# Interleaving the two matrix products of an expert loop on TensorE

## What is computed

```
glog = xf @ Wg + bg            ; 2 of 4 groups are kept
elog = xf @ We + be            ; 4 of 8 experts are kept in each group
h = gelu(xf @ W1[g] + b1[g])   ; 192 -> 768
o = h @ W2[g] + b2[g]          ; 768 -> 192
y = y + o * combine            ; sum over the experts that a token chose
```

## Time and profile before

| what | value |
|---|---|
| median of 3 runs | 839.55 us (836.72 to 843.9) |
| profiled execution, own time | 850.15 us |
| its span | 848.3 us |
| PE busy in the span | 722.8 us (85%) |
| expert loop, first product to the last | 452.08 to 839.01 us of the span |

### The profile page before, as it was taken

One profiled execution on the slowest core, in us unless ns is written; L12 is line 12 of the kernel. 1 busy time (PEld: TensorE's weight loads), 2 busy tenths in 40 slices (PEclk: granted clock), 3 DMA queues, 4 the chain that ended last, 5 costly groups with the idle time before them and its releaser, 6 DMA issues.

```text
span 848.3 us, 19851 instructions
## 1 busy us (share of the span) xinstructions
PE 722.8 (85%) x6412; PEld 603.1 (71%) x6412; DVE 397.9 (47%) x1167; ACT 239.4 (28%) x672; POOL 299.2 (35%) x259
## 2 busy tenths in 40 slices
PE   4967958788978999787267999999999999999995
PEld 4944645546663598575236888889889988898895
DVE  5657445653564714894892333333333333333332
ACT  2102212122415401111232333333333333333332
POOL 0122016021022420261003545545545555464554
PEclk9977867768976899796567999999999999999998
DMA  8940000000000002003112574546454556545422
GB/s 214 232 87 2 1 3 2 2 1 3 1 1 0 1 2 113 0 1 112 26 36 88 168 234 114 138 107 162 98 155 103 157 154 165 147 103 154 106 45 40
DMA packets 35163, 69.49 MB, mean 82 GB/s; under 512 B 6598, under 2 KB 21543, under 8 KB 35111
## 3 DMA queue, kind: packets, MB, share of 16 engines
q0 software_dynamic: 15840, 17.71, 12.2%
q10 hardware_dynamic: 8352, 34.30, 11.7%
q1 hardware_dynamic: 10919, 16.74, 7.5%
HBM read 58.75 MB, written 9.98 MB: 81 GB/s over the span
## 4 chain that ended last, share of the span: by engine, by line
PE 57%; DVE 16%; DMA 11%; issue 8%; POOL 2%; ACT 2%; POOLq 1%; ACTq 0%; DVEq 0%; SPq 0%
PE bank L1475 11%; PE bank L1467 9%; DMA arena<-normed_rows,fetch_u 7%; PE bank L1470 6%; PE bank L1250 4%; DMA out_dram<-arena,number_u 3%; PE bank L1324 3%; PE bank L1204 3%; PE bank L1452 2%; PE bank L1339 2%; PE bank L1363 2%; PE bank L1270 2%; PE bank L1208 1%; PE bank L1317 1%; PE bank L1298 1%
## 5 line engine op out<-in xcount | busy, mean ns | idle before, releaser
L618 POOL DMA_INDIRECT out_dram<-arena,number_u x80 | 127.1, 1588 | 31.6 <-issue 21.4
L612 POOL DMA_INDIRECT arena<-normed_rows,fetch_u x80 | 78.3, 979 | 150.3 <-DMA out_dram<-arena,number_u 54.2
L1169 DVE COPY arena<-bank 128x256 f32<-128x256 f32 x81 | 34.4, 424 | 161.9 <-PE bank L1452 146.6
L784 ACT ACTIVATE arena<-bank,arena 128x128 f32<-128x128 f32 x234 | 66.0, 373 | 123.3 <-PE bank L1470 110.7
L1475 PE MATMUL bank<-arena 128*128 128x192 f32 x468 | 85.4, 329 | 4.0 <-DVE arena L1189 2.8
L1475 PEld LDWEIGHTS bank<-arena 128*128 128x128 f32 x468 | 75.0, 190 | 7.3 <-ACT arena L784 3.7
L524 POOL TENSOR_SCALAR rstd<-mv 128x4 f32<-128x4 f32 x12 | 2.7, 228 | 201.7 <-DVE mv L860 201.7
L1467 PE MATMUL bank<-arena 128*128 128x128 f32 x468 | 60.4, 279 | 0.9 <-issue 0.2
L1467 PEld LDWEIGHTS bank<-arena 128*128 128x128 f32 x468 | 56.2, 191 | 5.7 <-issue 4.7
L784 ACT ACTIVATE arena<-bank,w_space 128x128 f32<-128x128 f32 x132 | 37.3, 373 | 72.6 <-PE bank L1470 71.8
L552 POOL TENSOR_TENSOR arena<-arena,v_space 128x2304 f32<-128x2304 f32 x8 | 34.5, 4316 | 55.4 <-DVE arena L1108 50.1
(11 more groups left out here) (237 smaller groups left out, 1265.5 us busy)
## 6 DMA issues: line engine op xcount, KB each, us to landing
arena<-in_moe_w_dram ACTq DMA_DIRECT2D x15, 579.0 KB
arena<-in_moe_w_dram ACTq DMA_DIRECT2D x15, 576.0 KB
w_space<-in_moe_w_dram ACTq DMA_DIRECT2D x7, 579.0 KB
w2small<-in_moe_w_dram ACTq DMA_DIRECT2D x7, 579.0 KB
w_space<-in_moe_w_dram ACTq DMA_DIRECT2D x7, 576.0 KB
wab<-in_moe_w_dram ACTq DMA_DIRECT2D x7, 576.0 KB
arena<-in_xf_dram SPq DMA_DIRECT2D x8, 480.0 KB, 15.8
arena<-in_w_dram SPq DMA_DIRECT2D x8, 450.0 KB, 14.2
```

What stands on the lines that cost most here:

```text
L612: pool.indirect_dma_start(out=mo_stage[:, s * ROWN:(s + 1) * ROWN], out_offset=None, in_=normed_rows, in_offset=bass.IndirectOffsetOnAxis( ...
L618: pool.indirect_dma_start(out=out, out_offset=bass.IndirectOffsetOnAxis(ap=number_u[:, s:s + 1], axis=0), in_=mo_res[:, s * D:(s + 1) * D] ...
L784: nc.scalar.activation(mo_hT[:, m, :], bank[2 + m][:, 0:P], ACT.Gelu, bias=b1[:, m:m + 1]).then_inc(free[2 + m], 1)
L1169: nc.vector.tensor_copy(mo_xT.rearrange("p k t -> p (k t)"), bank[1][:, 0:2 * P]).then_inc(free[1], 1)
```

## The change

One step of PE's loop handles two tiles: the second products of tile i-1, placed between the first products of tile i. Six second products, three before the first products and three among them; the 64-row products, which were six in one row, come in three pairs (m = 0,1; 2,3; 4,5), each pair behind full-height products. The first step multiplies a cleared `mo_hT` (POOL clears it before the loop), and six second products stand behind the last step. As tile i-1 may belong to the expert before, the second weights of the four places become one tile, `mo_w2_all`, and the place is added from a register of PE, `w2_at`. The loads of the weights move from ACT's queue to SP's and go when the last tile of the expert before has had its second products. At the beginning the second weights of experts 0 and 1 are loaded later, since their new place is used by the third attention until then. ACT loses one wait and DVE waits for one more count of `full[0]`.

```
-        mo_w2 = [w2_space[:], w2small[:, 0:W2N]] + [view(P, W2N) for _ in range(2)]
+        mo_w2_all = view(P, AHEAD * W2N)
+        mo_w2 = [mo_w2_all[:, u * W2N:(u + 1) * W2N] for u in range(AHEAD)]
...
             for u in range(2):
-                load_expert(sp, u, u)
+                load_first(sp, u, u)
             was_read(sp, "D", "proj", T - 1)
-            load_expert(sp, 2, 2)
+            for u in range(AHEAD):
+                if u >= 2:
+                    load_first(sp, u, u)
+                load_second(sp, u, u)
...
+            sp.wait_ge(sem("table_ready"), 1)
+            for e in range(1, NE - AHEAD + 1):
+                first = expert_start(sp, e, 1)
+                sp.wait_ge(full[0], first + (moe_base[0] + 1))
+                sp.sem_inc(sem("loading"), 1)
+                load_first(sp, (e - 1) % AHEAD, e + AHEAD - 1)
+                load_second(sp, (e - 1) % AHEAD, e + AHEAD - 1)
...
+            was_read(pool, "D", "proj", T - 1)
+            nc.gpsimd.memset(mo_hT.rearrange("p m t -> p (m t)"), 0.0).then_inc(sem("hidden_clear"), 1)
...
-                    act.wait_ge(full[0], first + moe_base[0])
-                    load_expert(act, (u + AHEAD - 1) % AHEAD, e + AHEAD - 1)
...
-                    act.wait_ge(full[0], i + moe_base[0])
...
-                    added, summing = dve.snap(i + 1), dve.snap(i + (moe_base[0] + 1))
+                    added, summing = dve.snap(i + 1), dve.snap(i + (moe_base[0] + 2))
...
+            def second(m):
+                rhs = mo_w2_all[:, bass.ds(pe.snap(w2_at, min_val=0, max_val=(AHEAD - 1) * W2N) + m * D, D)]
+                ins = mm(bank[0][:, 0:D], mo_hT[:, m, :], rhs, start=(m == 0), stop=(m == MC - 1))
+                if m == MC - 1:
+                    ins.then_inc(full[0], 1)
+
+            def first_rows(w1e, m):
+                mm(bank[2 + m][:, 0:P], w1e[:, m * P:(m + 1) * P], mo_xT[:, 0, :], start=True, stop=False)
+
+            def last_rows(w1e, m):
+                for q in (m, m + 1):
+                    r, c = q % 2 * REST, HID + q // 2 * P
+                    mm(bank[2 + q][:, 0:P], w1e[r:r + REST, c:c + P], mo_xT[r:r + REST, 1, :], start=False, stop=True).then_inc(full[2 + q], 1)
...
+                pe.reg_mov(w2_at, (e - 1) % AHEAD * W2N if e else 0)
                 with pe.Fori(first, end) as i:
+                    pe.wait_ge(free[0], i + (moe_base[0] - 1))
+                    for m in range(3):
+                        hidden_read(i, m)
+                        second(m)
                     pe.wait_ge(free[1], i + (moe_base[1] + 1))
...
+                    first_rows(w1e, 0)
+                    first_rows(w1e, 1)
+                    last_rows(w1e, 0)
+                    hidden_read(i, 3)
+                    second(3)
+                    first_rows(w1e, 2)
+                    hidden_read(i, 4)
+                    second(4)
+                    first_rows(w1e, 3)
+                    last_rows(w1e, 2)
+                    hidden_read(i, 5)
+                    second(5)
+                    first_rows(w1e, 4)
+                    first_rows(w1e, 5)
+                    last_rows(w1e, 4)
                     transpose_rows(i + 1)
...
+                    pe.reg_mov(w2_at, u * W2N)
```

More of the change, by code:

```diff
@@ L396, in vit_tower, with load_first, load_second @@
         halves = "(k p) n -> p k n"
[L398 to L402, removed]
+        def load_first(eng, u, e):
+            eng.dma_start(mo_w1[u], a["moe_w1"][bass.ds(e, 1)].rearrange("o p n -> p (o n)")).then_inc(sem(f"in_expert{u}"), 16)
+        def load_second(eng, u, e):
+            eng.dma_start(mo_w2[u], a["moe_w2"][bass.ds(e, 1)].rearrange("o p n -> p (o n)")).then_inc(sem(f"in_expert{u}"), 16)
         def expert_start(eng, e, least):
@@ L1453, in transpose_rows, with hidden_read @@
                 ins.then_inc(full[1], 1)
[L1455 to L1457 removed]
+            w2_at = pe.alloc_register("second_weights")
+            def second(m):
[9 more added lines that the diff above has]
+                    mm(bank[2 + q][:, 0:P], w1e[r:r + REST, c:c + P], mo_xT[r:r + REST, 1, :], start=False, stop=True).then_inc(full[2 + q], 1)
+            def hidden_read(i, m):
+                pe.wait_ge(free[2 + m], i + moe_base[2 + m])
             def expert(e, first, end):
@@ L1461, in expert @@
                 w1e = mo_w1[u]
-                w2e = mo_w2[u][:, 0:MC * D].rearrange("p (m d) -> p m d", m=MC)
                 pe.wait_ge(sem(f"in_expert{u}"), 32 * (e // AHEAD + 1))
+                pe.reg_mov(w2_at, (e - 1) % AHEAD * W2N if e else 0)
                 with pe.Fori(first, end) as i:
+                    pe.wait_ge(free[0], i + (moe_base[0] - 1))
+                    for m in range(3):
+                        hidden_read(i, m)
+                        second(m)
                     pe.wait_ge(free[1], i + (moe_base[1] + 1))
[L1466 to L1470, removed]
-                    transpose_rows(i + 1)
[L1472 to L1479, removed]
+                    first_rows(w1e, 0)
[13 more added lines that the diff above has]
+                    last_rows(w1e, 4)
+                    transpose_rows(i + 1)
+                    pe.reg_mov(w2_at, u * W2N)
+            pe.wait_ge(free[1], moe_base[1])
+            pe.wait_ge(sem("table_ready"), 1)
             first, end = expert_start(pe, 0, 0), expert_start(pe, 1, 1)
+            transpose_rows(0)
+            pe.wait_ge(sem("hidden_clear"), 1)
             for e in range(NE):
@@ L1484, in _ @@
                 first, end = end, after
+            pe.wait_ge(free[0], first + (moe_base[0] - 1))
+            for m in range(MC):
+                hidden_read(first, m)
+                second(m)
         for k, v in lots.items():
```

1 line of the change is left out of this document (removed).

## The result

The changed kernel takes **923.3 us** (median of 4 runs, 922.93 to 927.19) against 838.1 us (836.18 to 843.9) before: a ratio of 1.0995, 95% interval 1.0935 to 1.1055. The profiled execution has a span of 921.2 us; before it was 848.3. I had forecast 884 us and a range of 862 to 908. The direction was right, but the time lies outside the range: the forecast rise of 44 us is about half of the 85 measured.

The account below looks back on a forecast made before the run. PE bounds the expert loop: a 4.53 us floor per step plus 21.7 us of waiting. Round trips +60, waits -21.7, six extra products +1.95 and registers +4 give +44 us, from 839.55 to 884 us; range 862 to 908.

Parts of the forecast that it names:

- Order of PE's products: PE's step: three round trips between 128 and 64 rows instead of one, two more at 0.38, +0.76 us a step.
- Rivals 1 and 2: PE's height changes: round trips free, 820 us (chance 0.08), or partly hidden at 0.08 to 0.18, about 840 (0.05).
- Register address: PE's second weights: register copied and added to six times a step, 0.05 us a step, 4 us; bounds 0 to 20.
- Waits that go: PE's loop: waits for ACT and at changes of expert vanish, all 21.7 us gone; lower bound 16.9.
- The wait for bank 0: Start of PE's step: margin for DVE's scaling shrinks from 1.9 to 0.3 us but holds; second products cover columns.
- A late DVE: DVE's waits for `result_free`: could add up to 22.7 us on PE; taken as 0, kept for the range.
- rival 3: Bank 0 late, DVE's waits reach PE, registers cost 0.25 a step: 923 at most, 903 with half; chance 0.15.
- First and last step: Loop's ends: six zero products in the first step taken as 0, plus or minus 1; six behind the last, +1.95 us.
- The sum: Whole kernel: +44 us, profile 850.15 to 894; median kept 10.6 below the profile, 839.55 to 884 us.

Follow-up runs that it names:

- e4: Kernel before with only its first products reordered into three groups of four 128-row and two 64-row products, three round trips a step; 890.0 us, ratio 1.0537.
- e6: Kernel before with its six 64-row products using all 128 rows, a changed computation; 849.4 us, one run.
- e2: Changed kernel with the three groups of 64-row products together behind first product 5, one round trip a step; 849.2 us, ratio 1.0010.
- e9: Kernel before with four result buffers instead of two and nothing else; 835.2 us, ratio 0.9968.
- e8: Changed kernel with `starts` read early, 64-row products in one group, four result buffers and POOL's wait for accumulation moved later; 830.2 us, ratio 0.9886.
- e12: e8 unchanged, run again beside e11 on the same chip; 832.5 us, ratio 0.9912.
- e1: Changed kernel, but DVE reads the next expert's bound in `starts` once per tile, where it idles, and hands it on in registers; 892.1 us, ratio 1.0559.
- e11: Changed kernel with `starts` read early and 64-row products in one group, still two result buffers; 839.2 us, ratio 1.0002.
- e5: e1 with second weights at the current expert's address without a register, so first tiles after expert changes use wrong weights; 885.9 us, one run.

## Why the prediction was wrong

*Order of PE's products.* Right. Forecast +0.76 us a step for two round trips; e4 measured 0.79, which is 62 us of the change, and e6 confirmed the cause. Rivals 1 and 2, with cheap round trips, are out. The floor of the changed kernel was forecast at 5.34 with the register, and is 5.36.

*Register address.* Right in size: 0.05 forecast, 0.06 measured with three round trips, and nothing with one (e2).

*Waits that go.* Right: the 22 us went, though the 29 places that I called "as many as there are changes of expert" are two short of the 31. But e4 shows that they go in the old order as well once the step is longer, so in the changed kernel they say nothing for the interleaving. At steps of 4.53 us it does hide waits: with four result buffers the old order keeps an excess of 10.6 us (e9), the interleaved one 5.3 and 2.2 (e8, e12, which also read `starts` early).

*The wait for bank 0.* This is the step that failed: in it I put the wait of PE for the columns at nothing. I wrote that the margin at bank 0 "holds for a punctual DVE" and that for the columns "three second products, 0.98 us, now cover them". I took the time of the copy after the transposes from an ordinary step and did not list what else stands in DVE's program between scaling and the copy: at each change of expert the end of two loops and two reads of `starts`. In the old order scaling came just after the step began and the columns in its middle, so this work fell into DVE's idle time. The trace of before shows both, the reads (by source line) and the copy behind them, in the step of the earlier trace rows:

```profile
L1176 DVEq TENSOR_LOAD <-starts x32: 312/318/562, 451.7 to 826.8; - x32
```

```profile
607.47 0.42 DVE L1169 COPY arena<-bank 128x256 f32<-128x256 f32 x1 [2.79 <-PE bank L1452]
```

The idle time of 2.79 us is put down to PE, since the transposes (606.35) end last, and the reads of 604.92 to 606.24 are hidden in it; a list of waits doesn't show them. In the new order scaling starts at 605.27, 0.7 us before the step's transposes are through, and the columns are due at about 607.0, 1 us behind them. In these 1.7 us the sequencer's 2.2 and the copy's 0.43 don't fit, and PE lost 1.02 us in 31 steps, 31.7 us. e1 gave 30.1 us of it back (455.0 to 424.9 for the 79 steps).

*A late DVE, rival 3.* I gave 0.15 to a late DVE and had its mechanism half: the new place of scaling leaves no slack. The cause I named, the landing of the accumulating DMA, was not the one that struck here; it was too quick for steps of 5.4 us, as I had argued. It did strike at steps of 4.53 (e11), where it cost 9 us in the traces and 6.8 in the times, about the whole gain of e12. That the measured 923.3 meets the outer end of this rival, 923, is luck: its terms were 22.7 us for landings and 16 for registers, and the runs show 31.7 for DVE's sequencer, some 5 for the register, and the 10 of the baseline below.

*First and last step.* Taken as 0, the first step became 1.8 us longer. What it lasts depends on the clock: PE idles before it, and it begins at a granted clock of 0.50. In e1 it takes 8.93 us, in e5 7.28. The first part of each, e1 and then e5, with its granted clock in the third column from the end:

```profile
443.34:450.10 6.76, 6.28 (x22) 5.44 (x23) 0.87 (x4) 0.62 (x2) 2.59 (x3) 0.50 0.12 34
```

```profile
445.38:448.80 3.42, 3.16 (x10) 2.77 (x11) 0.87 (x4) 0.00 (x0) 1.53 (x2) 0.50 0.12 34
```

In e1 the lower clock lasts 3.3 us longer, and at half the clock that costs about the 1.65 us between the two steps. In the trace of before the whole first step ran at 0.50, in that of the changed kernel 6.9 of its 9.05 us. So the added 1.8 us hold the six products with zeros and two round trips, mostly at the lower clock; what each of them cost there was not measured.

*The sum.* I carried the profile's 10.6 us above the median through to the changed kernel. Its profile lies at its median instead. Of the 39 us by which I was short, 10 are of this baseline and remain unexplained (the runs beside the changed kernel have a median of 838.1, 1.4 below the one I used). The other 29 lie in the traces (+44 forecast, +72.9 found): the new wait 31.7, the first step 1.8, the floor 1.6, less some 6 ahead of the loop and behind it.

## What to carry to other kernels

Read the intervals between the starts of matmuls where one height of the array follows another: here each trip to 64 rows and back costs 0.39 us, as much as three and a half float32 matmuls of 128 columns, so products of one height belong together; by e6's step of 4.85 us full height is cheaper than three groups of pairs and dearer than one. When an operation moves within a loop, list for every other engine what its program has between the two operations that now stand close together, sequencer work at the outer loop's edge included, and not only what it has in an ordinary step. And a step at its floor exposes the next queue: the interleaving paid only after the 64-row products, DVE's registers and the result buffers had been put right (e12: 0.9%). The kernel before with both of the last two edits was not run; against e9, which has the buffers alone, the interleaved kernel is 0.6% faster.

## What the runs showed of the hardware

At 2.4 GHz a float32 product of 128 columns is two matmuls of 0.112 us each and one of 192 columns two of 0.163. Six pairs on 64 rows start 7 ns apart within the pair and 0.112 from pair to pair. Between heights the interval is 0.205 going to 64 rows and 0.202 coming back, and the first interval after either change is 0.10 too long (0.06 where the way back ends in the transposes); in the traces these numbers vary by less than 0.01 us in nine of ten places. Reading one number from SBUF into a register of DVE takes about 0.3 us for the load and 0.2 for what follows it: DVE's two reads and the edges of two loops made 1.8 us of its idle time. After PE had been idle for 2.6 us in e11, its granted clock was 0.50 for 3.4 us, and the step lasted 1.8 us longer than the wait explains.
